# A graph and feed-forward kernel on one core: the row of numbers that one-hots are compared with moves from SBUF to PSUM

## Time and profile before

| what | value |
|---|---|
| median of 3 runs | 5961.54 us (5959.02 to 5963.64) |
| profiled execution | 5950.92 us |
| its span | 5949.1 us |
| mean granted clock of TensorE | 0.904 of full speed |
| POOL busy | 4087.5 us (69%), 4176 of its instructions are indirect DMAs |
| DVE busy | 4196.2 us (71%) |
| costliest group of POOL | L623, 2568 gathers of the layers, 2454.3 us |
| L590, gathers of the attention | 808, 798.3 us |
| L581, scatters | 680 from `acc_mem` (708.6 us), 120 more from other places |

### The profile page before, as it was taken

The page is one execution under the profiler, slowest core; times in us unless marked ns, Lnnn a source line. Parts: engine busy times, 40 slices in busy tenths (PEclk is TensorE's granted clock), DMA queues, the critical chain, the costliest instruction groups (busy, mean ns, idle before and its releaser), DMA issues.

```text
span 5949.1 us, 89553 instructions
## 1 busy us (share of the span) xinstructions
PE 4487.4 (75%) x25082; PEld 2797.4 (47%) x25082; DVE 4196.2 (71%) x9654; ACT 2286.6 (38%) x5880; POOL 4087.5 (69%) x4202
## 2 busy tenths in 40 slices
PE   6459987899888876777777767777776777777787
PEld 2135544666666644444444434444444444444455
DVE  8789986777777654666766757777675777777734
ACT  0038875555555523333333323333332223232321
POOL 1467777777777777777777757777776777777700
PEclk9579998888898888999999989999999999999979
DMA  5011111434333313444444434444444444445400
GB/s 149 19 40 29 29 26 37 108 107 107 106 102 101 93 35 111 135 135 129 133 133 131 134 104 139 139 138 139 139 139 117 137 139 138 140 138 140 137 25 22
DMA packets 445005, 624.93 MB, mean 105 GB/s; under 512 B 97099, under 2 KB 330261, under 8 KB 444564
## 3 DMA queue, kind: packets, MB, share of 16 engines
q0 software_dynamic: 187648, 457.52, 27.7%
q1 hardware_dynamic: 250164, 159.14, 9.5%
q10 hardware_dynamic: 6754, 2.96, 0.2%
HBM read 556.32 MB, written 62.94 MB: 104 GB/s over the span
## 4 chain that ended last, share of the span: by engine, by line
PE 25%; DVE 14%; issue 11%; POOL 10%; ACT 2%; DVEq 2%; DMA 1%; POOLq 0%; ACTq 0%; SPq 0%
PE banks L1173 13%; DVE acc_mem L1692 6%; POOL sort_mem L623 6%; DVE z_mem L1835 5%; PE banks L1203 4%; POOL recB_d L581 3%; PE banks L1161 2%; PE banks L1106 1%; PE banks L1116 1%; DMA sort_mem<-x_d,x_mem 1%; DVEq L1681 1%; DVEq L1692 1%; ACT z_mem L809 1%; PE banks L1158 1%; PE banks L1193 1%
## 5 line engine op out<-in xcount | busy, mean ns | idle before, releaser
L623 POOL DMA_INDIRECT sort_mem<-x_d,x_mem x2568 | 2454.3, 956 | 877.7 <-issue 764.3
L1173 PE MATMUL banks<-z_mem 128*128 128x257 f32 x5136 | 1567.7, 430 | 903.9 <-DVE acc_mem L1692 766.8
L1173 PEld LDWEIGHTS banks<-z_mem 128*128 128x128 f32 x5136 | 850.5, 199 | 1601.3 <-ACT z_mem L809 718.4
L1692 DVE TENSOR_TENSOR acc_mem<-acc_mem,banks 128x257 f32 x2568 | 1081.8, 421 | 556.0 <-PE banks L1173 383.0
L809 ACT ACTIVATE z_mem<-z_mem 128x512 f32<-128x512 f32 x1284 | 768.8, 628 | 1375.6 <-DVE z_mem L1835 1375.6
L1835 DVE TENSOR_TENSOR z_mem<-banks,sort_mem 128x512 f32<-128x512 f32 x1284 | 825.4, 685 | 412.3 <-PE banks L1161 301.6
L581 POOL DMA_INDIRECT recB_d<-acc_mem,sort_mem x680 | 708.6, 1042 | 410.6 <-DVE sort_mem L1423 205.4
L590 POOL DMA_INDIRECT acc_mem<-h_d,xnt_mem x808 | 798.3, 988 | 246.1 <-issue 235.5
L1049 PE MATMUL banks<-acc_mem,xnt_mem 128*128 128x257 f32 x1616 | 579.3, 483 | 44.0 <-DVE acc_mem L1635 41.8
L1635 DVE SCALAR_TENSOR_TENSOR acc_mem<-acc_mem,z_mem,banks 128x257 f32 x808 | 386.7, 479 | 114.8 <-PE banks L1049 100.4
L1161 PE MATMUL banks<-z_mem,x_mem 32*128 32x256 f32 x5136 | 422.1, 404 | 0.0
(11 more groups left out here) (355 smaller groups left out, 5714.1 us busy)
## 6 DMA issues: line engine op xcount, KB each, us to landing
x_mem<-recB_d SPq DMA_DIRECT2D x642, 68.0 KB
sort_mem<-x_d,x_mem POOLq DMA_INDIRECT x2568
x_mem<-at_d SPq DMA_DIRECT2D x428, 64.0 KB
at_d<-x_mem SPq DMA_DIRECT2D x214, 64.0 KB
acc_mem<-h_d,xnt_mem POOLq DMA_INDIRECT x808, 2.8
x_mem<-x_d SPq DMA_DIRECT2D x100, 128.0 KB, 2.5
acc_mem<-in_edge_attr SPq DMA_DIRECT2D x40, 312.5 KB
recB_d<-acc_mem SPq DMA_DIRECT2D x3, 3672.0 KB, 26.1
```

What stands on the lines that cost most here:

```text
L623: pool.indirect_dma_start(out=xg[h % XG][:, k, :], out_offset=None, in_=x_ds[l % 2], in_offset=bass.IndirectOffsetOnAxis(ap=reci[h][:, k, ...
L1173: m.matmul(bank[5 + tile % 2][:, :AC], oneh[:, Q % 2, k, :], msg[:, Q % 2, k, :], start=True, stop=True)\
L1692: v.tensor_tensor(a_, a_, bank_[:, :AC], ALU.add).then_inc(flushed, 1)
```

## The change

Bank 7 gets the row of numbers at the start, by one copy. The three comparisons L1399, L1532 and L1572 read it there (fp32) in place of `iota_b` (bf16, SBUF). As TensorE writes late ranks into the same bank, the one-hots of an attention step wait first until the late rank of the step before is written (`rankedB`); this is 28 waits.

```diff
@@ build @@
         turned_ps = bank[2].bitcast(BF16)
+        numbers = bank[7][:, 3 * P:4 * P]
@@ VectorE, start @@
             dve.wait_ge(S("p_const"), 14 + len(late_recs))
+            st.did(v.tensor_copy(numbers, iota))
             st.did(v.tensor_scalar(ident, iota, iota_col, None, ALU.is_equal))
@@ late_onehot @@
-                io = iota_b[:EP, 0:BKT_B].rearrange("p (a b) -> p a b", a=1).broadcast_to([EP, 5, BKT_B])
+                io = numbers[:EP, 0:BKT_B].rearrange("p (a b) -> p a b", a=1).broadcast_to([EP, 5, BKT_B])
@@ hot_columns @@
-                v.tensor_tensor(lone[:, h, :, :], iota_b[:EP].rearrange("p (a s) -> p a s", a=1).broadcast_to([EP, 4, P]),
+                v.tensor_tensor(lone[:, h, :, :], numbers[:EP].rearrange("p (a s) -> p a s", a=1).broadcast_to([EP, 4, P]),
@@ one_hots @@
-                v.tensor_tensor(seg1[:, o % 3, :, :], iota_b.rearrange("p (a s) -> p a s", a=1).broadcast_to([P, 8, P]),
+                v.tensor_tensor(seg1[:, o % 3, :, :], numbers.rearrange("p (a s) -> p a s", a=1).broadcast_to([P, 8, P]),
@@ attention steps, VectorE @@
                 if s_ < OCTS:
+                    for g in late:
+                        if s_ > late_step(g):
+                            dve.wait_ge(S("rankedB"), g + 1)
                     one_hots(s_)
```

## The result

The changed kernel takes 5928.67 us, the median of five runs (5918.99 to 5932.51), against 5963.64 us (5959.02 to 5966.57) for the kernel before, measured beside it. The ratio is 0.9939 (95% interval 0.9925 to 0.9954), so the change brings 36 us by the ratio, between 27 and 45. The forecast was 5919, with 5909 to 5941 as its range. The profiled execution took 5918.99 us with a span of 5917.2, 31.9 less than the span before. It is the quickest of its five runs; the profiled execution of before, with 5950.92 us, is 8 us quicker than the quickest of the five measured of that kernel.

What follows compares the result with a forecast made beforehand. POOL was taken to bound the kernel from 397.2 to 2326 us. Terms of -33.9, -11.3 and +2 gave -43 us, from the profiled 5950.92 to 5908; with 10.6 more for the median, 5919 us, range 5909 to 5941.

Steps and rivals of the forecast that it cites:

- (1): One-hots of attention: with numbers in bank 7 the 42 ns excess on 808 gathers goes, -33.9 us.
- (2): The comparisons' own time: reading from a bank costs between -2 and 0 ns each, taken as 0.
- Rival D: Slower: comparisons mixing fp32 bank numbers with bf16 get long, at half rate about 6130 us in all; chance 0.04.
- (3): Placing: scatters lose 15.1 us of collisions, but gathers need L1561's output at 1007.4; first gather 11.3 us earlier.
- (4): Attention: the 28 waits on `rankedB` ahead of the one-hots are over when reached, 0 us.
- (5): Start: copying 128 numbers to bank 7, some 0.3 us, is covered by the wait for the ids, 0 us.
- (6): Attention's consumers: at 10.00 us an octet against POOL's 10.01 they sometimes hold POOL up, +2 us, bounds 0 and 8.
- A: The forecast itself: collisions go and POOL's savings shorten the kernel to 5919 us, own range 5911 to 5929; chance 0.78.
- rival B: Attention: the consumers bound it, so less is gained; between 5933 and 5950 us, put at 5936; chance 0.11.
- (7): Behind attention: the 200 scatters and the feed-forward part move along with it, nothing given back.

Runs made afterwards that it cites:

- e1: Kernel before with only the one-hots of attention (L1572) reading bank 7, placing and late ranks left in SBUF; ratio 0.9968 to the kernel before.
- e2: Kernel before with only the comparisons of placing and late ranks reading bank 7, attention left in SBUF; ratio 0.9988 to the kernel before.
- e3: Kernel before with all three comparisons reading fp32 numbers in SBUF in place of bf16, nothing in PSUM; ratio 1.0004 to the kernel before.
- e5: Changed kernel with 84 small waited-for memsets added on POOL during placing; one execution, no kernel time given, `recI` ready at 1027.3 us in place of 992.6.
- e6: Kernel before with only the late-rank comparisons reading bank 7, placing and attention in SBUF; one execution, no kernel time given, scatters' mean 1020 ns.
- e8: The changed kernel, unaltered, run again beside the version with one-hots moved ahead of the maxima; 5925.87 us, ratio 0.9936 to the kernel before.
- e4: Changed kernel with the one-hots of attention and their wait moved ahead of the maxima of the same step; ratio 0.9913 to the kernel before.
- e9: Changed kernel with one-hots and their wait ahead of the maxima, run again beside the changed kernel; 5915.12 us, ratio 0.9921 to the kernel before.
- e7: Kernel before, all numbers in SBUF, with only the one-hots of attention moved ahead of the maxima; ratio 1.0007 to the kernel before.

## Why the prediction was right, and where it was not

The claim, that the change takes away collisions by which VectorE holds POOL up, and that POOL is what bounds this part of the kernel, is shown: e1 and e2 each give their part, e3 shows that width isn't the cause, and the gathers' longest time falls from 1997 to 979 ns. By its steps:

(1) -33.9 us for the gathers' excess: POOL's busy time in attention fell from 798.3 to 765.0, by 33.3. Right.

(2) The comparisons' time: right, 0 to -3 ns each. Rival D is out. The rule of the Trainium skill that a PSUM operand costs a tier (VectorE: DVE Perf Modes, The perf-mode tier table) had nothing to take here: the comparison took the same 1218 ns with two bf16 inputs in SBUF, and e3 and the change agree with 1219 and 1217 ns. Why it was not quicker from SBUF no run shows. What the term left out is the 4.8 us by which the tensor_scalars of placing got longer.

(3) -11.3 us for placing: -13.8 in the profile, 12.4 of them from placing and 1.4 from its earlier start. The number is close by luck, for the way to it was wrong. The sum took `recI` as ready at 1007.4, "from the placing matmuls and not from POOL", and so let it cut 15.1 us to 11.3. It moved by 14.8 us, to 12.7 us ahead of the first gather; POOL's extra 16.4 us in e3 moved it by 15.2, and POOL's 36.6 us in e5 by 34.7. So in these runs POOL's scatters bound placing: they took 13.3 us less, and one wait for addresses took 1.0 us more. The row that said it, ScalarE's 61 to 69 us on the scatters, was at hand.

(4) and (5), wait and copy at nothing: right. The 28 waits are of 21 ns, and VectorE never stood idle ahead of the comparison behind them. The copy took 0.29 us at 10.81, and VectorE still waited 4.25 us for the ids behind it.

(6) +2 us for the consumers: this term was mis-sized. The stretch is 1019.8 us against 1011 of POOL alone, so it is about 9 us. I had the consumers' own pace from the profile before, 10.00 us an octet; without waiting for rows they take 1027.71 to 2031.34 for 99 octets, 10.14 us each. A reserve of 0.01 us an octet was no reserve, and the pace itself was too low: the sum took every wait for rows as time that the consumers would give back. The same subtraction gives 9.87 to 10.02 us in the four executions of this order with collisions (before, e2, e3, e6), and 10.13 to 10.15 in e1, the changed kernel and e8, where there is next to nothing to subtract. Part of A and part of rival B are therefore true: POOL stands behind L1050 in 46 places, up to 1.5 us, as B said it would show. e4 shows that it is the consumers: nothing but the place of the one-hots in their step differs, and the 10 us come back. Why they are slower than they were when they waited now and then isn't settled. The granted clock of TensorE was 0.85 of full speed in this stretch before, 0.83 after and 0.90 in e9, a mixture of 1.2 and 2.4 GHz, and L1050 has a mean of 498 ns on the page where L1049 had 483; that goes with it, but no run changed the clock alone.

(7) "Nothing given back": right. Layer 0 starts 38.2 us earlier, which is what placing and attention brought, 13.8 and 24.4 us. The 1.9 us of slower landing were made good by scatters that took 2.0 us less from the last gather on.

The forecast has layer 0 starting 43.2 us earlier: attention gave 7.5 us less than its two terms, placing 2.5 more. For the median the forecast was 42.5 us of gain, and 35 came by the medians. The rest of the distance between 5919 and 5928.7 lies in the comparison: the five runs of the kernel before have their median 2.1 us above the 5961.54 that the forecast started from. In (1) and (2) and in the claim the prediction was right by its mechanism; that 5928.7 is inside 5909 to 5941 owes something to the width of the range, as one term had its cause wrong and another its size. A's own range doesn't follow from its bounds either: those of (3) and (6) give 5913 to 5936 and not 5911 to 5929.

## What to carry to other kernels

Where POOL issues indirect DMAs on the critical path, keep long two-input VectorE instructions from having both inputs in SBUF: one of them in a PSUM bank cost these comparisons nothing, at 1.04 ns an element as from SBUF, and their neighbours 4.8 us. Look at the distribution of POOL's instruction times, not at their mean, and match the long ones by start time to what VectorE was doing. And once one engine of two with equal pace is freed, the other one is the bound at once: look for what in its loop can stand elsewhere before counting the whole gain.

## What the runs showed of the hardware

A POOL instruction is held up only if it starts while the comparison is already running. In the kernel before, 102 gathers start inside an L1572. 87 of them are lengthened (82 by over 30 ns, which are those that the prediction counts) and end 0.81 to 0.82 us after the comparison; the others start in its first 0.02 us, or so late that their usual 0.95 us end after that point anyway. One that has started ahead of it, if only by 10 ns, takes its usual time: 88 gathers overlap a comparison in this way, and the longest takes 956 ns (1507.54 in the earlier trace rows is one).

The Trainium skill says that VectorE and GpSimd share one pair of ports by an exclusive lock (SBUF — State Buffer, Who interferes with whom). The trace agrees where POOL is the later one, 1.23 against 0.95 us in the earlier trace rows. The other way round it shows no such wait for the comparison, which keeps its 1217 to 1220 ns in 86 of the 88 cases where a gather is already running (1248 at most).

With the 512-element comparison of placing in a bank it is some of the tensor_scalars that get longer: 28 to 40 of 800 take over 560 ns in each execution with that change (e5 apart, with 82), and none does in before, e1, e3, e6 and e7. In the changed kernel all 31 start 0.49 to 0.56 us into a scatter; those that start earlier in one keep their 420 ns. Why isn't settled.

Where the comparisons and the tensor_scalars follow each other without a gap, a scatter can wait through several: 2.54 us at 522.71, 2572 ns at most. With the first of the chain out of SBUF (e6) the most is 1512 ns, and with both comparisons out of it 1402 to 1742. The four tensor_scalars of L1536 go on costing POOL 20 to 25 us in all versions; nothing was tried against that.

How much the collisions cost depends on how the two engines' beats lie against each other, and differs from execution to execution of the same comparisons: 28 to 46 us in attention, scatters of 1040 to 1076 ns in placing. One profile is one draw from that; the table above has the range.
